# FFN block of a one-core megakernel: where ScalarE squares the third and fourth query/key unit of the next row

## What is computed

```
x = x + 0.5 * ffn(layernorm(x))          # "ffn0", the block of this change
x = x + attention16(layernorm(x))        # 16 heads of 8
x = x + 0.5 * ffn(layernorm(x))          # "ffn1", the same function, same weights
x = x + 0.5 * mixture_of_experts(layernorm(x))
x = x + test_time_training(layernorm(x))
x = x + 0.5 * mixture_of_experts(layernorm(x))
```

```
h = shift_token(y)                       # upper 64 features from the token before
q, k, v = split(h @ wqkv, 3)             # 8 heads of 64
q = q / |q| * q_scale ; k = k / |k| * k_scale       # norm per head and token
q = q*cos*s + rotate_half(q)*sin*s ; k likewise with 1/s
o = local attention in windows of 64 keys back, softmax
y = y + o @ wo
h = layernorm(shift_token(y)) * g + b
a, g = split(h @ w1 + b1, 2) ; y = y + (a * gelu(g)) @ w2 + b2
```

## Time and profile before

| what | value |
|---|---|
| median of 3 runs | 2515.07 us (2504.59 to 2523.34) |
| the profiled execution: time | 2525.46 us |
| its span, first to last instruction | 2523.6 us |
| mean granted TensorE clock | 0.879 |
| TensorE matmul busy | 1966.8 us, 78% |
| VectorE busy | 1579.5 us, 63% |
| ScalarE busy | 1237.9 us, 49% |
| GpSimd busy | 1052.1 us, 42% |

### The profile page before, as it was taken

One profiled execution on the slowest core, in us unless ns is written; L12 is line 12 of the kernel. 1 busy time (PEld: TensorE's weight loads), 2 busy tenths in 40 slices (PEclk: granted clock), 3 DMA queues, 4 the chain that ended last, 5 costly groups with the idle time before them and its releaser, 6 DMA issues.

```text
span 2523.6 us, 43414 instructions
## 1 busy us (share of the span) xinstructions
PE 1966.8 (78%) x14880; PEld 1231.2 (49%) x14880; DVE 1579.5 (63%) x2479; ACT 1237.9 (49%) x2826; POOL 1052.1 (42%) x838
## 2 busy tenths in 40 slices
PE   2788888759898896589888873796687888884696
PEld 1555555424555554355555542683344644642485
DVE  6677777557979976667777746584443344335486
ACT  2465656447979975465565544243322222234242
POOL 2455555335767765354555515232231033003333
PEclk9899999976979978698899995898799999896798
DMA  6000000020000001000000012204000000000202
GB/s 212 1 1 1 2 2 1 2 88 13 22 18 24 22 21 41 0 2 1 2 1 2 2 47 82 58 23 142 0 0 0 1 0 0 0 0 13 66 22 66
DMA packets 43928, 63.32 MB, mean 25 GB/s; under 512 B 7504, under 2 KB 33488, under 8 KB 42736
## 3 DMA queue, kind: packets, MB, share of 16 engines
q1 hardware_dynamic: 39232, 51.96, 6.7%
q0 software_dynamic: 4544, 9.35, 1.2%
HBM read 45.26 MB, written 21.18 MB: 26 GB/s over the span
## 4 chain that ended last, share of the span: by engine, by line
issue 31%; PE 17%; DVE 4%; ACT 3%; DMA 1%; POOL 1%; SPq 1%; DVEq 0%; POOLq 0%; ACTq 0%
PE PS L1723 3%; PE PS L1705 2%; PE PS L1707 1%; PE PS L1706 1%; PE PS L448 1%; PE PS L1713 1%; DVE arena L757 1%; ACT arena L635 1%; DVE arena L770 1%; PE PS L471 1%; PE PS L412 1%; PE PS L500 1%; PE PS L318 1%; ACT arena L619 1%; DMA arena<-sorted_x 1%
## 5 line engine op out<-in xcount | busy, mean ns | idle before, releaser
L1497 POOL TENSOR_TENSOR arena<-arena 128x1024 f32<-128x1024 f32 x128 | 300.0, 2365 | 144.0 <-ACT arena L1431 144.0
L949 POOL TENSOR_TENSOR arena<-arena 128x512 f32<-128x512 f32 x128 | 138.9, 1087 | 249.6 <-DVE arena L791 247.9
L757 DVE SCALAR_TENSOR_TENSOR arena<-PS,fcol,big 128x512 f32<-128x512 f32 x256 | 178.9, 745 | 99.4 <-ACT arena L611 92.6
L635 ACT ACTIVATE arena<-PS,arena 128x128 f32<-128x128 f32 x512 | 180.7, 370 | 119.1 <-DVE arena L784 118.7
L318 PE MATMUL PS<-arena_r 128*128 128x512 f32 x216 | 126.5, 586 | 126.6 <-DVE arena L757 56.5
L1405 PE MATMUL PS<-con,arena 128*128 128x128 f32 x1024 | 163.5, 307 | 45.6 <-DVE arena L1481 44.2
L1405 PEld LDWEIGHTS PS<-con,arena 128*128 128x128 f32 x1024 | 124.4, 155 | 121.3 <-issue 96.6
L1431 ACT ACTIVATE arena<-PS,arena 128x512 f32<-128x512 f32 x256 | 155.1, 688 | 56.2 <-DVE arena L1462 54.5
L1481 DVE COPY arena<-PS 128x512 f32<-128x512 f32 x256 | 166.4, 685 | 24.8 <-PE PS L1405 24.4
L1442 ACT ACTIVATE arena<-arena 128x512 f32<-128x512 f32 x256 | 162.6, 636 | 23.3 <-DVE arena L1469 17.2
L1462 DVE TENSOR_REDUCE arena<-PS 128x4 f32<-128x2048 f32 x64 | 146.7, 2292 | 29.3 <-PE PS L1387 29.3
(11 more groups left out here) (366 smaller groups left out, 4897.6 us busy)
## 6 DMA issues: line engine op xcount, KB each, us to landing
big<-in_gu SPq DMA_DIRECT2D x16, 512.0 KB, 8.0
sorted_x<-in_slots SPq DMA_DIRECT2D x2, 2515.5 KB, 14.2
arena<-sorted_x SPq DMA_DIRECT2D x6, 774.0 KB, 7.2
big<-in_dn SPq DMA_DIRECT2D x16, 256.0 KB, 8.4
arena<-expert_y SPq DMA_DIRECT2D x16, 256.0 KB, 3.3
big<-in_wqkv SPq DMA_DIRECT2D x2, 1536.0 KB, 8.5
arena<-q_split SPq DMA_DIRECT2D x96, 32.0 KB
arena<-k_split SPq DMA_DIRECT2D x96, 32.0 KB
```

Of the source, the lines that this page charges most:

```text
L635: act.activation(pr[:, u % 2, t, :], PS[:, u % 2, t * P:(t + 1) * P], ACT.Exp, bias=nmax[:, u % 2, t:t + 1], accum_out=psum_[:, u % 2, t:t ...
L757: v.scalar_tensor_tensor(t_prod[:, j % 2, 2 * half + i, :], PS[:, pair_bank(r, j) + half, :], fcol[:, layer, kind + half:kind + half + 1], ...
L949: g.tensor_tensor(pn[:, u % 2, :, :], pr[:, u % 2, :, :], pinv[:, u % 2, :].unsqueeze(2).broadcast_to([P, TPB, P]), ALU.mult).then_inc(s(" ...
L1497: g.tensor_tensor(a, a, mk[:, hp, 2 * half:2 * half + 2, :], ALU.mult).then_inc(s("a_masked"), 1)
```

## The change

In ScalarE's list of a transition `square(2)` moves from behind `norm(1)` to ahead of it, and `square(3)` moves from behind `norm(2)` to ahead of `take_heads(r, 3)`. Nothing is added or taken away, no wait and no other engine's list is altered.

```diff
@@ -698,11 +698,11 @@
                 square(1)
                 exponentials(r, 7)
                 take_heads(r, 2)
+                square(2)
                 norm(1)
-                square(2)
+                square(3)
                 take_heads(r, 3)
                 norm(2)
-                square(3)
                 if nx is not None:
                     hidden_input(r)
                     exponentials(nx, 0)
```

## The result

| kernel | median, us | runs from | to | ratio to before, 95% interval |
|---|---|---|---|---|
| before | 2517.48 | 2504.59 | 2523.34 | |
| changed | 2452.86 | 2436.80 | 2463.68 | 0.9743 [0.9706, 0.9780] |

The change is faster by 2.6%, 65 us. The forecast was 2452.

What follows compares the result with a forecast made beforehand. No engine is full; a chain of waits, chiefly VectorE's for late ScalarE squares, bounds the 14 transitions. 240.90 - 14 x 12.74 saves 62.5 us, from the median 2515.07 to 2452; range 2432 to 2482.

Steps and rivals of the forecast that it cites:

- The two waits: VectorE's waits for a square in rotations 2 and 3, 2.11 and 4.11 us, both go.
- Scaling 0 held once: VectorE's scaling of unit 0 meets GpSimd's add of unit 2's squares and waits for it: 0.86 us lost.
- Scaling 1 and 2: VectorE's next scalings also meet GpSimd: scaling 1 takes 2.27 us, scaling 2 takes 2.36 as before.
- The end of the transition: Maxima start at 178.67 instead of 183.21; a transition from norm(1)'s old start lasts 12.74 instead of 17.28 us.
- TensorE's tail: Attended and scores end last, maxima at 178.67; as rival, low clock there costs up to 25 us (0.16, shared with more turns).
- VectorE's tail: Scalings, then the addition to y at 177.03, make the maxima due at 178.45, 0.2 us before TensorE's.
- Project 3: On TensorE, starts at 167.29, 2.13 us earlier; 2.85 us from its start to values 3 kept.
- I take nothing back later.: Next row's work all stands behind the same maxima and addition, so none of the 62.5 us is lost afterwards.
- The clock: TensorE's gap before project 3 shrinks from 3.09 to about 1 us, so project 3 runs at full clock.
- The turns: Rival: VectorE scalings and GpSimd held by turns; milder form 2467 to 2482 (0.16, shared), slower, 2535 (0.02).
- That nothing changes: Rival: something else binds VectorE at the same time, so time stays 2515 us; 0.06, shared with turns eating nearly all.

Runs made afterwards that it cites:

- g1: Kernel before with only square 2 moved ahead of norm(1), square 3 left behind norm(2): 2458.50 us, ratio 0.9765.
- g2: Kernel before with only square 3 moved ahead of take_heads 3, square 2 left behind norm(1): 2468.97 us, ratio 0.9809.
- k2: Changed kernel plus one extra, unread GpSimd add of unit 2's squares in each of the 14 transitions: 2472.72 us, ratio 0.9830.
- k3: Changed kernel without GpSimd's adds of squares; TensorE sums both squares itself for all units: 2448.62 us, ratio 0.9746.
- g3: Changed kernel with take_heads 3 ahead of square 3 instead of behind it: 2442.19 us, ratio 0.9703.
- m1: Changed kernel unaltered, measured again on another chip beside the kernel before: 2443.05 us, ratio 0.9725.
- m2: Repeat of g3 on the same chip as m1: 2438.87 us, ratio 0.9685.
- k1: Kernel before plus three unused float32 matmuls in TensorE's gap ahead of project 3: 2505.59 us, ratio 0.9969.

## Why the prediction was right, point by point

**The two waits.** Right. Rotation 2 and rotation 3 each run as four products without a gap, and project 3 starts 163.40 - 160.55 = 2.85 us after rotation 2 (predicted 167.29 - 164.44, the same). g1 and g2 show that each wait goes with its own move.

**Scaling 0 held once.** Right in size: predicted 2.11 us, measured 2.13; k2 doubled it and k3 removed it.

**Scaling 1 and 2.** Predicted 2.27 + 2.36 = 4.63, measured 4.63. In the second transition the add of unit 3 held the second of the four instructions, in the 13 others the third; I had it hold the first. The sum is the same, since the add and the first half of rotated 3 each hold one scaling, whichever it is.

**The end of the transition.** Predicted 178.67 - 164.44 = 14.23 us from the start of rotation 2, measured 14.02 in the second transition, 14.04 on average. The difference, 0.2, lies on TensorE's tail, which I had called the later one: attended began 7.93 us after rotation 2, not 8.20, and the scores ended 13.97 us after it. VectorE's tail I had at 178.45 - 164.44 = 14.01 us, and that is what it measured. So the two tails end together, and g3, which takes TensorE's 1 us forward, shortens nothing. That makes the predicted saving 62.5 us against 65.2.

**Project 3.** I kept 2.85 us from its start to values 3, a length at the lower clock, and forecast the full clock for it further on. It took 1.58 us. The 1.3 us cost the forecast nothing, because the heads wait for the second square of unit 3 and that waits 1.60 us for VectorE; I had the heads wait only 0.4 us.

**"I take nothing back later."** This step failed. I wrote that all of the next row hangs on the maxima and the addition to y, and stopped at the maxima. TensorE's sums 3, values and mean for the next row stand behind the same late attended. They now come 1.0 us later against the maxima than with the heads first (g3), and the row pays 0.33 us on average. 495.92 - 491.37 = 4.6 us of the gain went there in this pair of traces, 3.7 in m1 and m2. It is a loss against the kernel before too: the stretches behind its third and fourth transition, at the full clock throughout, took 34.59 us each, nearly as in g3 (34.57), and 34.97 in the changed kernel. The sum before is larger all the same, 500.7, because low stretches of the clock fell into other rows of it.

**The clock.** The full clock on project 3 was predicted. What I did not count is that low stretches can turn up elsewhere. In the first profile of the changed kernel, the two last rows took 46.1 and 43.4 us, together 10.6 more than before. From first rotation to last hidden_input the two blocks went from 450.5 + 452.9 to 423.9 + 420.1: 59.4 us saved, which is 65.2, plus 4.8 in the stretches between, less the 10.6. The rest of the program, which the change does not touch, took 8 us less (1620.2 and 1612.1 us). So the agreement of the medians to 1 us is partly luck: beside the kernel before on another chip (m1) the same change gained 73 us. The agreement within the transition is not luck; it came out at 14.03 to 14.06 us again in m1.

**The rivals.** TensorE's tail did not lengthen the transition but does cost a little in the next row; that the low clock can fall on it is real (k2), but it did not here. The turns took what I had counted in the transition and no more. That nothing changes is refuted.

## What to carry to other kernels

In a list that an engine executes strictly in order, an instruction whose operands are ready goes ahead of one that still waits for another engine's round trip. Ask first who stands still for it. When such a wait goes, follow every engine past the point where the first one is satisfied: here VectorE's gain was whole, but TensorE, held up by the same reordering, handed a third of a microsecond back one row later. And a list that now runs tight makes two engines meet that had taken turns by accident; count one hold for each instruction of the other engine that falls beside it.

## What the runs showed of the hardware

A VectorE instruction with both inputs in SBUF (L770, 680 ns alone) and a GpSimd add (1.27 us alone) hardly overlap. The one that comes second waits for the other to end: the scaling takes 1.53 us behind an add already under way, about 1.75 when it must wait out nearly all of one. It goes both ways: in 13 transitions of the changed kernel the add of unit 3 is shown 0.02 or 0.03 us ahead of two scalings, which went first, and took 2.42 us. An extra add of GpSimd costs VectorE 1.08 us even where GpSimd itself had idle time to spare. That is the rule of "SBUF — State Buffer", Who interferes with whom, in the Trainium skill, and k2 and k3 bear it out. The rule there has a condition that the prediction left out: an instruction with one SBUF input is free of GpSimd only outside VectorE's two-port performance modes, which `copy` can enter. This case has a copy that was held, of y into h2 right before the maxima. In the changed kernel GpSimd's L943 still runs for its first 0.50 us; in k3 GpSimd is idle there (shown above, L805: 0.42 us):

```profile
173.81 0.78 DVE L804 COPY arena<-arena 64x512 f32<-64x512 f32 x1
```

It takes 0.77 to 0.79 us in all 14 transitions, before and after the change, and 0.42 in the last rows, where GpSimd is idle too.

The low clock moves. TensorE's gap of 3.09 us stood in all 14 transitions of the kernel before, and 11 of them had a stretch at half the clock. Filling it, by work or by useless matmuls, took the low clock from project 3. In the changed kernel it left the transitions; in k1 it came back in the scores of 5, behind a gap of 1.57 us. In k1 and in both profiles of the changed kernel it then appeared in the blocks' last rows, where the kernel before had run at the full clock (and g3's first profile nearly so: 39.4 and 40.1 us). First the kernel before, then the changed one:

```profile
455.51:494.90 39.39, 32.87 (x401) 20.05 (x399) 21.09 (x38) 22.13 (x80) 13.59 (x15) 1.00 0.01 2
```

```profile
422.28:468.34 46.06, 40.17 (x399) 24.27 (x402) 21.42 (x38) 22.52 (x81) 13.29 (x15) 0.81 0.01 2
```

The same work takes 6.7 us more at a mean clock of 0.81. In the changed kernel's other profile these rows took 42.5 us each. g1 had one of these rows at 39.4 us and the other at 42.2, so it is no property of a kernel's order alone. Why the last rows and not others stays open; nothing here was tried on it.

The part of the program that no experiment touched took between 1598 and 1620 us in the profiles. The changed kernel alone had 1612.1 us in its first and 1598.7 in m1. The kernel before's only profile had the longest, 1620.2; g1 and g2 had 1601.2 and 1602.6. That is as much as the 11 to 12 us by which my expectations for g1 and g2 were too high while their transitions came out as expected, but I made these expectations from medians, and what moved the medians is not shown.
